# When the DMA-issuing queue of a two-layer transformer kernel starts its q and k loads: position -7 against position -12

## The reference

```
h = layernorm(x) * (1 + ca) + sa
x = x + ga * attention(h)          # 16 heads of width 8; layer 0 adds slopes[h] * (k - q) to the scores
h = layernorm(x) * (1 + cb) + sb
x = x + gb * experts(h)            # 16 experts of width 64, the best 2 per token; layer 1 adds a shared expert
```

## Time and profile before

| | |
|---|---|
| median of 3 runs | 1702.93 us |
| the profiled execution | 1702.93 us, its span 1701.2 us |
| busy, share of the span | PE 80%, DVE 76%, ACT 64%, POOL 60% |
| instructions | PE 14409 matmuls, DVE 3854, ACT 2558, POOL 1416 |
| moved by DMA | 283.04 MB, mean 166 GB/s |

### The profile page before, as it was taken

How to read it: one execution, slowest core, us unless ns; L and a number is a source line. 1 busy time by engine, 2 the same in 40 slices (tenths; PEclk the granted TensorE clock), 3 DMA queues, 4 the chain that set the end, 5 groups by cost and what they waited for, 6 DMA issues and landing times.

```text
span 1701.2 us, 45413 instructions
## 1 busy us (share of the span) xinstructions
PE 1354.3 (80%) x14409; PEld 836.5 (49%) x14409; DVE 1300.5 (76%) x3854; ACT 1087.4 (64%) x2558; POOL 1012.4 (60%) x1416
## 2 busy tenths in 40 slices
PE   2488888888888878888999889988889868875631
PEld 1144444445555545554556555655556535544531
DVE  5479998788887897879988898898988857743422
ACT  1188887677777776767777667776777656642321
POOL 1223334833585777577876678576865783686573
PEclk9999999899999998989999999999999989987766
DMA  3665766566677776776777667677667765656763
GB/s 90 151 149 150 161 151 144 139 157 160 173 187 176 176 174 175 184 170 166 188 170 177 152 162 183 166 186 175 170 181 188 181 177 142 176 166 172 214 196 100
DMA packets 447673, 283.04 MB, mean 166 GB/s; under 512 B 33773, under 2 KB 436751, under 8 KB 447439
## 3 DMA queue, kind: packets, MB, share of 16 engines
q1 hardware_dynamic: 412334, 237.12, 56.6%
q0 software_dynamic: 16384, 33.59, 7.1%
q10 hardware_dynamic: 18720, 9.44, 1.9%
HBM read 171.75 MB, written 108.18 MB: 165 GB/s over the span
## 4 chain that ended last, share of the span: by engine, by line
POOL 26%; PE 23%; DVE 23%; issue 17%; DMA 5%; ACT 3%; SPq 2%; POOLq 0%; DVEq 0%; ACTq 0%
DVE mx L1657 10%; POOL slot_dram L696 8%; POOL y_in L717 5%; PE ps_job L1109 5%; PE ps_s L1243 3%; PE ps_q L1082 3%; POOL ln_rs L662 2%; DMA k_stk<-part_dram 2%; DMA h_blk<-slot_dram 2%; POOL qk_part L743 2%; POOL qk_rest L739 2%; PE ps_q L1065 1%; POOL x L729 1%; PE ps_job L1130 1%; PE ps_q L1097 1%
## 5 line engine op out<-in xcount | busy, mean ns | idle before, releaser
L1657 DVE TENSOR_REDUCE mx<-ps_s 128x2 f32<-128x512 f32 x1024 | 655.2, 682 | 112.6 <-PE ps_s L1243 110.8
L894 ACT ACTIVATE prob<-ps_st 128x512 f32<-128x512 f32 x1024 | 557.1, 595 | 90.6 <-PE ps_st L1249 87.8
L1243 PE MATMUL ps_s<-k_stk,q_stk 51*128 51x256 bf16 x2048 | 361.0, 282 | 138.3 <-DVE mx L1657 68.3
L1249 PE MATMUL ps_st<-q_stk,k_stk 53*128 53x256 bf16 x2048 | 355.2, 281 | 6.6 <-ACT prob L894 6.3
L1109 PE MATMUL ps_job<-prob,v_ext 128*32 128x256 f32 x4096 | 291.1, 404 | 27.2 <-issue 10.0
L1243 PEld LDWEIGHTS ps_s<-k_stk,q_stk 51*128 51x128 bf16 x2048 | 141.6, 96 | 334.5 <-DVE mx L1657 198.5
L696 POOL DMA_INDIRECT slot_dram<-h_row,slot x256 | 255.8, 999 | 71.0 <-issue 65.4
L717 POOL DMA_INDIRECT y_in<-y_dram,slot x224 | 222.8, 995 | 77.6 <-issue 51.0
L836 ACT ACTIVATE o_sb<-ps_job 128x256 f32<-128x256 f32 x256 | 97.0, 379 | 173.0 <-PE ps_job L1109 169.0
L1109 PEld LDWEIGHTS ps_job<-prob,v_ext 128*32 128x32 f32 x4096 | 116.5, 113 | 131.6 <-issue 36.9
L739 POOL TENSOR_TENSOR qk_rest<-qk_f,qk_part 128x512 f32<-128x512 f32 x64 | 74.5, 1164 | 160.6 <-ACT qk_part L927 160.3
(11 more groups left out here) (206 smaller groups left out, 2642.2 us busy)
## 6 DMA issues: line engine op xcount, KB each, us to landing
w_q<-in_we SPq DMA_DIRECT2D x376, 128.0 KB
h_blk<-slot_dram SPq DMA_DIRECT2D x50, 512.0 KB, 5.2
part_dram<-qk_part SPq DMA_DIRECT2D x128, 192.0 KB
q_stk<-part_dram SPq DMA_DIRECT2D x128, 192.0 KB
k_stk<-part_dram SPq DMA_DIRECT2D x128, 192.0 KB
y_dram<-y_sb SPq DMA_DIRECT2D x46, 512.0 KB, 3.2
part_dram<-qk_part SPq DMA_DIRECT2D x128, 128.0 KB
mod_in<-row_dram SPq DMA_DIRECT2D x64, 192.0 KB
```

The source lines that it names most:

```text
L894: sc.activation(prob[:, (k ^ 1) % 8, :], ps_st[k % 2][:], ACT.Exp).then_inc(exp_done, 1)
L1243: mm = pe.matmul(ps_s[j % 2][:, t * S:(t + 1) * S], q_stk[us.tri][r0:r0 + R_BIAS, hp, t * P:(t + 1) * P], k_stk[us.tri][r0:r0 + R_BIAS, hp ...
L1249: mm = pe.matmul(ps_st[k % 2][:, t * S:(t + 1) * S], k_stk[ut.tri][r1:r1 + R_MAX, hp, t * P:(t + 1) * P], q_stk[ut.tri][r1:r1 + R_MAX, hp, ...
L1657: dve.tensor_reduce(mx[:, hp // 4, :, 4 * par + hp % 4], ps_s[j % 2][:].rearrange("p (t s) -> p t s", s=S), AX_X, ALU.max).then_inc(max_do ...
```

## The change

`stack_rows(u)` is issued at position -12 of its unit, where it stood at position -7. Nothing else is edited.

```diff
@@ -570,7 +570,7 @@
                 u = at(step, -17)
                 if u:
                     part_rows(u)
-                u = at(step, -7)
+                u = at(step, -12)
                 if u:
                     stack_rows(u)
                     if u.no in (B, B + 1, B + 2):
```

## The result

| | before | after |
|---|---|---|
| median | 1699.95 us (20 runs) | 1710.12 us (20 runs, 1701.49 to 1716.84) |
| ratio | 1 | 1.0059, 95% interval 1.0042 to 1.0078 |
| the profiled execution | 1702.93 us, span 1701.2 | 1714.06 us, span 1712.0 |

The forecast was 1693.5 us. A later set of runs of the changed kernel gave 1.0037 (1.0011 to 1.0062).

The account below looks back on a forecast made before the run. No engine alone sets the pace; POOL, PE and DVE share the chain. 1702.9 - 8.5 (start) - 5.0 (six waits) + 1.5 (maxima) + 2.6 (unit 63) = 1693.5 us; own range 1687 to 1700, 8 in 10 1684 to 1710.

Parts of the forecast that it names:

- The start: Unit 0's stack no longer goes out behind `setup()`, so unit 1 starts earlier: 8.5 us gain (bounds 7.1 and 14.05).
- the maxima's second half: Its store goes out behind the stack and SyncE waits at L500, delaying its loads: 1.5 us cost (bounds 0 and 30).
- What else waits behind the stack now: `mod_in`, the next unit's parts, some `gate_b` and `quad_load` issues in SyncE's queue: all counted at nothing.
- unit 63: Three weight loads and the y store move behind its stack, weights 3 us late: 2.6 us cost (bounds 0 and 5).
- The six waits: PE's 7.3 us of waits for stacks in units with expert work go; two thirds counted, 5.0 us gain.
- Rival 1: The start gives 8.5 us, but the six waits become others and queue blocking costs 4.5 us: 1698.9 us, chance 0.22.
- Rival 3: Behind the stack, the maxima's store and then loads land one after the other, costing 28 us: 1722 us, chance 0.14.
- The reading of the 1.2 us: SyncE's wait for the maxima's store, taken as its landing time with nothing large ahead, against the skill's 2.0 us.
- Rival 2: All is gained: unit 1 not late at its stack, the six waits counted in full, nothing lost: 1681.6 us, chance 0.12.

## Why the prediction was wrong

- **The start** was right in its mechanism and too small: 11.0 us in the trace, 11.4 us alone, for 8.5.
- **That a stack moves only past what SyncE did in front of it**, since it waits for PE's step -7, was right (9.4 and 9.5 us ahead of unit 48's scores).
- **The step that failed** is in the part on the maxima's second half: "What else waits behind the stack now [...] I count these at nothing". I let the parts of unit u+1 be late by up to 1 us "with a stack behind them that waits for PE anyway", and named the block loads of units 19, 23, 27, taken by PE 12 steps later. I missed the load that stands right behind `part_rows`: the first of each group, with next to no slack in the kernel before (PE stood 1.3, 0.2 and 2.0 us for three of the six; the others had at most some 0.7 us to spare, an estimate: PE came 4.7 us after the issue at block groups 18 and 24, where it didn't wait, and 4.0 at block group 0, where it did). It came 2.9 us later at unit 48, and 0.6 to 3.6 at the others. In place of nothing the term is 11 us (16.5 for the later stacks less unit 63's 5.4), as far as the runs can tell: with early loads nothing measurable is left.
- The working had priced each item by its own wait. But SyncE's waits at L521 and L500 add up in one queue, and the sum shows first where the queue used to have slack, at L510 (264.1 to 52.7 us). The forecast had the growth of both waits right (L521 over 100 us, L500 4 us behind a stack) and did not follow it to the next row.
- **The six waits** went as forecast, from 7.3 us to none, but were worth nothing measurable in sum rather than 5.0. Rival 1's doubt was right as far as the runs can tell.
- **The maxima's second half** cost 0 to 1.0 us of PE's waits in the two profiles, for 1.5. Rival 3, the only one on the slower side, did not come: the rows were there in time in every unit of one profile, and all but two (1.0 us in sum) of the other. Its sign came true by another mechanism, so that it pointed the right way was luck.
- **The reading of the 1.2 us** was wrong. It is an average of SyncE's waits and not the time from issue to landing, and 53 of the 63 waits are for the first half's store, which goes out right behind the parts of a unit, six DMAs and 768 KB (192, 128 and 64 KB, each twice; not 1.15 MB), so not with nothing large ahead. From the end of the store's issue to its landing these waits show 1.0 to 3.4 us, 1.8 on average. The estimate of 2.0 us that the prediction takes from the Trainium skill (DMA: Bandwidth & Descriptors, "Anatomy of one DMA — SWDGE (gpsimd) path") lies inside that, so the trace doesn't disagree with it; and that section is on DMAs that GpSimd issues, not on SyncE's. The reason given for leaving it out of rival 3's chance doesn't hold.
- **Unit 63** was too small: 5.4 us, and 10.3 in one profile, for 2.6. The weights took 7.2 us from issue to PE, for the 4 to 5 assumed.
- **`gate_b`**, also counted at nothing, is waited for by GpSimd, 3.6 us in 6 waits; no run shows what that costs.
- **Rival 2** fell at the start already: unit 1 did wait for its stack, 2.71 us.
- **The range** was added up too narrowly: the upper bounds of the start, the six waits and unit 63 (1.4, 5.0 and 2.4 us) give 1702.3, not 1700.
- **Rival 1** named `h_blk` and unit 63 among what gives the gain back, at 4.5 us in all; the measured cost is about four times that.
- What no term held is the clock: behind some of the waits of 2 to 5 us PE runs at the half level (1.97 for 1.09 us), and on average over the runs the granted clock is 0.929 for 0.935. What this adds to the cost of an idle microsecond stays open.

The sum with measured terms: -11.4 for the start, nothing for the six waits, +5.4 for unit 63 and +11.1 for the block loads (16.5 for all later stacks), thus 5 us slower; the direct measurements are 6 and 10 us.

## What to carry to other kernels

When a waiting DMA issue moves up in a queue, it gains nothing beyond what it waited behind, and all that it passes is late by the wait. List every load behind it up to the next point at which the queue itself waits for another engine; that wait is the slack, and once it is used up the first load behind it needs a price, by how long it lands before its reader asks. Move what has no slack ahead of what can wait: here six loads two steps earlier took back all that the stacks of units 1 to 62 had measurably cost.

## What the runs showed of the hardware

- An 8 KB store of the maxima in SyncE's queue, where SyncE waits for it: with 768 KB of stores just ahead, it had landed 1.0 to 3.4 us after the end of its issue (53 waits of the kernel before, mean 1.8); behind a stack of 768 KB of loads 2.7 to 6.0 us (62 waits of the kernel after, mean about 4.5). In the kernel before the stack was issued right behind this second store, and its issue covered about 2 to 3 us of the same time, so SyncE waited for it in ten units only, 0.7 us each.
- PE ran the same eight 128x128 f32 matmuls (L1065) in 1.09 us, and in 1.97 after standing 2.67 us, with a granted clock of 0.73 over the 12 us that follow. It didn't always fall at once: in the two profiles of the changed kernel they took 1.97 us after idle times of 2.53, 2.67, 2.79, 3.02, 4.77 and 4.80 us, and 1.09 or less after 2.08, 2.26, 2.33 and 2.51. After the 2.26 the clock fell later in the stretch (0.86).
- Moving one small DMA issue per unit from SyncE to ACT, 0.31 us each and a wait for ACT's own copy, cost 18 us over 64 units, 0.28 us per unit.
